# A sandwich layer of linear attention and a mixture of experts on one core: GpSimd's double power behind the fourth key sums, VectorE's x_mid behind the candidate mask and xn1

## What is computed

```python
# block 1: linear attention in chunks of 128, mixed with a memory
q, k, v = h @ w_q.T, h @ w_k.T, h @ w_v.T
sq, sk = elu(q) + 1, elu(k) + 1
mem   = (sq @ memory) / clip(sq @ memory_norm, EPS)
A     = (sq_chunk @ sk_chunk.T) * causal
local = (A @ v + sq_chunk @ S) / clip(A.sum(-1) + sq_chunk @ z, EPS)   # S += sk.T @ v, z += sk.sum
out   = (g * mem + (1 - g) * local) @ w_o.T
# block 2: 1024 experts chosen by product keys, 4 heads, 8 of them each, and a dense part
sim           = queries of h against 64 keys a side and head
sx, sy        = top 8 of each side;  scores = top 8 of the 64 sums sx + sy
w             = silu((h . down_embed[idx]) * softmax(scores))
out           = sum(w * up_embed[idx]) + silu(h @ W_up.T) @ W_down.T
```

## Time and profile before

| | us |
|---|---|
| median of 3 runs | 2862.96 |
| lowest, highest | 2859.02, 2871.89 |
| the profiled execution, its own time | 2859.55 |
| its span | 2857.8 |
| PE busy | 2784.0 (97%) |
| PEld busy | 2178.7 (76%) |
| DVE busy | 2624.6 (92%) |
| ACT busy | 2539.0 (89%) |
| POOL busy | 2064.3 (72%) |

### The profile page before, as it was taken

The page is one execution under the profiler, slowest core; times in us unless marked ns, Lnnn a source line. Parts: engine busy times, 40 slices in busy tenths (PEclk is TensorE's granted clock), DMA queues, the critical chain, the costliest instruction groups (busy, mean ns, idle before and its releaser), DMA issues.

```text
span 2857.8 us, 46700 instructions
## 1 busy us (share of the span) xinstructions
PE 2784.0 (97%) x13306; PEld 2178.7 (76%) x13306; DVE 2624.6 (92%) x6346; ACT 2539.0 (89%) x3692; POOL 2064.3 (72%) x2435
## 2 busy tenths in 40 slices
PE   8999999999999999999999999999999999999998
PEld 7677777777777777777777777777777777777776
DVE  6899899999999999999999999999999999999986
ACT  6888989899899898998998989989989889899997
POOL 5666677777777777777777777777777777777774
PEclk9999999999999999999999999999999999999999
DMA  4787888788878887888788778877887788788764
GB/s 133 151 168 159 170 170 170 162 173 172 168 161 175 167 172 158 174 172 168 160 176 171 165 166 173 169 164 168 171 173 162 169 173 173 159 176 171 147 152 117
DMA packets 609029, 471.49 MB, mean 165 GB/s; under 512 B 362371, under 2 KB 543492, under 8 KB 608772
## 3 DMA queue, kind: packets, MB, share of 16 engines
q0 software_dynamic: 52832, 199.77, 39.6%
q1 hardware_dynamic: 555940, 268.74, 38.3%
HBM read 137.37 MB, written 131.20 MB: 94 GB/s over the span
## 4 chain that ended last, share of the span: by engine, by line
DVE 46%; PE 19%; ACT 13%; issue 13%; POOL 8%; DVEq 0%; POOLq 0%; ACTq 0%
PE banks L873 17%; DVE sums L1402 5%; DVE banks L1405 4%; DVE prob_odd L1443 4%; DVE picked L1392 4%; DVE prob_odd L1549 4%; DVE w_blocks L1477 4%; DVE xn L1338 3%; POOL sums L696 3%; ACT L1190 3%; ACT prob_odd L1213 3%; DVE picked L1541 2%; POOL wexp L772 2%; DVE x_mid L1568 2%; DVE top L1492 1%
## 5 line engine op out<-in xcount | busy, mean ns | idle before, releaser
L696 POOL TENSOR_TENSOR sums<-scores 128x1024 f32<-128x1024 f32 x512 | 1066.4, 2085 | 327.6 <-ACT scores L1304 320.4
L873 PE MATMUL banks<-deT,xn2T 128*128 128x512 f32 x1024 | 481.9, 593 | 5.5 <-DVE wexp L1423 4.9
L873 PE MATMUL banks<-xn2T,wupT 128*128 128x256 f32 (+1 forms) x2272 | 465.3, 359 | 3.5 <-DVE state L1536 2.5
L873 PE MATMUL banks<-ue,gT 128*128 128x256 f32 x2048 | 462.9, 379 | 2.3 <-ACT gT L1234 2.3
L873 PEld LDWEIGHTS banks<-ue,gT 128*128 128x128 f32 x2048 | 388.8, 190 | 55.3 <-ACT gT L1234 2.7
L873 PEld LDWEIGHTS banks<-xn2T,wupT 128*128 128x128 f32 x2272 | 390.1, 191 | 46.6 <-DVE state L1536 3.3
L873 PEld LDWEIGHTS banks<-deT,xn2T 128*128 128x128 f32 x1024 | 184.6, 190 | 138.4 <-issue 123.4
L1549 DVE SCALAR_TENSOR_TENSOR prob_odd<-picked,rz,prob_odd 128x1024 f32<-128x1024 f32 x128 | 257.6, 2012 | 18.5 <-ACT prob_odd L1213 12.7
L1170 ACT ACTIVATE wexp<-prob_odd 128x1024 f32<-128x1024 f32 x127 | 134.2, 1057 | 154.1 <-DVE w_blocks L1477 153.7
L714 POOL TENSOR_TENSOR cprob<-cmask,cdif 128x112 f32<-128x112 f32 x128 | 58.7, 459 | 263.7 <-DVE cmask L1574 263.7
L873 PE MATMUL banks<-route,xn2T 128*128 128x512 f32 x512 | 240.8, 592 | 0.8 <-ACT xn2T L1134 0.8
(11 more groups left out here) (191 smaller groups left out, 7393.1 us busy)
## 6 DMA issues: line engine op xcount, KB each, us to landing
wexp<-wexp POOLq DMA_DIRECT2D x127, 1024.0 KB, 10.4
wexp<-wexp POOLq DMA_DIRECT2D x127, 512.0 KB, 5.2
w_way<-w_blocks SPq DMA_DIRECT2D x127, 512.0 KB, 3.1
g_parts<-w_way SPq DMA_DIRECT2D x508, 128.0 KB, 7.6
xn_way<-xn_blocks SPq DMA_DIRECT2D x992, 32.0 KB, 1.7
x_in<-_attn_hidden_states_dram SPq DMA_DIRECT2D x128, 128.0 KB, 5.9
out_dram<-x_out SPq DMA_DIRECT2D x128, 128.0 KB, 8.3
xn1T<-xn_way SPq DMA_DIRECT2D x125, 128.0 KB, 3.9
```

The lines of the kernel that those rows point to most:

```text
L696: return nc.gpsimd.tensor_tensor(sums[:, k, :, :], scores[:, k, 0:XIN].unsqueeze(2).broadcast_to([P, XIN, NKEYS]), scores[:, HEADS + k, :] ...
L873: last = nc.tensor.matmul(out, lhs(c), rhs(c), start=(start and c == 0), stop=(stop and c == chunks - 1), skip_group_check=shared)
```

## The change

On POOL the fourth sums (head 3) go ahead of the power and of its waits. On DVE the candidate mask and xn1 go ahead of x_mid. Computation, tiles and semaphores are the same.

```diff
--- before.py
+++ after.py
@@ -699,6 +699,8 @@
                                                ALU.add)
 
             def body(t, steady):
+                if t[9] is not None:
+                    key_sums(3).then_inc(s_head_3_sums_ready, 1)
                 if t[7] is not None:
                     pool.wait_ge(s_mix_var_eps, t[7] + 1)
                     if with_y(t[7]) is None:
@@ -706,8 +708,6 @@
                     else:
                         pool.wait_ge(s_y_var_eps, with_y(t[7]) + 1)
                         two_powers(2 * LN_O + t[7] % 2, 2 * LN_Y + with_y(t[7]) % 2).then_inc(s_mix_rstd, 1)
-                if t[9] is not None:
-                    key_sums(3).then_inc(s_head_3_sums_ready, 1)
                 if t[9] is not None:
                     pool.wait_ge(s_cand_exp_ready, t[9] + 1)
                     pool.wait_ge(s_cand_mask_ready, t[9] + 1)
@@ -1562,14 +1562,6 @@
                     x_moments(x)
                 if seven(t[13]) and t[13] % 2 == 0:
                     cross_added(t[13])
-                if t[7] is not None:
-                    dve.wait_ge(s_mix_rstd, t[7] + 1)
-                    wait(dve, s_x_out_ready, t[7] - MID_SLOTS + 1)
-                    nc.vector.scalar_tensor_tensor(x_mid[:, t[7] % MID_SLOTS, :], mix[:, 0:D], rstd[:, LN_O, t[7] % 2:t[7] % 2 + 1],
-                                                   x_in[:, t[7] % SLOTS, :], ALU.mult, ALU.add).then_inc(s_x_mid_ready, 1)
-                    if t[7] == 1:
-                        dve.wait_ge(s_ue_in, 16)
-                        nc.vector.reduce_sum(ue_sum[:, :], ue[:, :, :], axis=AX.X).then_inc(s_ue_cent, 1)
                 if t[9] is not None:
                     nc.vector.tensor_tensor(cmask[:, :, :], cand_out, per_head(best[:, :, TOP - 1], NCAND), ALU.is_ge).then_inc(s_cand_mask_ready, 1)
                 x = ahead(t, 4)
@@ -1587,6 +1579,14 @@
                         x_stats(x + 2)
                         x_moments(x + 2)
                         x_eps(x + 2)
+                if t[7] is not None:
+                    dve.wait_ge(s_mix_rstd, t[7] + 1)
+                    wait(dve, s_x_out_ready, t[7] - MID_SLOTS + 1)
+                    nc.vector.scalar_tensor_tensor(x_mid[:, t[7] % MID_SLOTS, :], mix[:, 0:D], rstd[:, LN_O, t[7] % 2:t[7] % 2 + 1],
+                                                   x_in[:, t[7] % SLOTS, :], ALU.mult, ALU.add).then_inc(s_x_mid_ready, 1)
+                    if t[7] == 1:
+                        dve.wait_ge(s_ue_in, 16)
+                        nc.vector.reduce_sum(ue_sum[:, :], ue[:, :, :], axis=AX.X).then_inc(s_ue_cent, 1)
 
             pipeline(body)
```

## The result

The changed kernel takes 2913.28 us (median of 4 runs, 2912.14 to 2916.21) against 2861.83 for the kernel before in the same comparison: ratio 1.0175, 95% interval 1.0149 to 1.0201. It is slower by 51 us, inside the range given (2822 to 2975), but not the forecast: it is rival 1 in its partial form. The profiled execution has a span of 2911.5 us at full granted clock; DVE is busy 2670.3 us (92%), POOL 2244.1 (77%), PE 2794.9 (96%).

A forecast was written before the change was run, and what follows sets the result against it. A loop through POOL's head-pair DMA (L772) was taken to bound the step, so DVE's -0.3 + 0.25 - 0.23 us hardly counts; 4 us off 2859.55 gives 2855.5, median 2859, forecast 2855. Range for 8 in 10: 2822 to 2975.

The forecast's parts named there:

- rival 1: DVE's x_mid is held by POOL's third sums: +190 us, about 3050, or near 2990; chance 0.28.
- partial form: x_mid is held by the third sums in some steps only: +20 to +110 us; a third of the 0.28.
- The loop through the DMA: POOL's head-pair DMA (L772) and its landing set the step; 0.15 us in two steps can go.
- the sum: Whole run: 0.15 us in two steps, about 55 times, 8 us at most, half taken: 4 us.
- (a): POOL's fourth sums ahead of the power shorten DVE's L1549: between 0 and -0.68 us, taken as -0.3.
- (c): DVE's L1402 moves later and no longer meets POOL's third sums: 0.23 us a step gained.
- (b): x_mid behind cmask and xn1 on DVE, with rstd ready: +0.1 to +0.3 us, taken as +0.25.
- The full one: x_mid is held by the third sums in every step: about 3050, or near 2990; chance 0.2.
- The Trainium skill's rule: DVE and POOL share a port pair; who starts first locks it; alone, the sum would be 87 us less.
- the signs named: Profile after: L1549 1.3 to 1.4 or near 2.0, L1402 1.27, `xn` above 0.6, L1063's wait 35 to 50 us.
- the two that the text called fatal: Forecast wrong if x_mid's mean exceeds 0.9 us or the two-step loop is outside 43.0 to 43.7.

The follow-up runs named there:

- experiment 6: The changed kernel with POOL's third sums waiting for x_mid and the DMA L772 over half its columns, against the kernel before: 2801.07 us, ratio 0.9783.
- experiment 3: The changed kernel with POOL's third sums made to wait for x_mid, against the kernel before: 2843.93 us, ratio 0.9949.
- experiment 4: The changed kernel with cmask behind xn1 on DVE (xn1, cmask, x_mid), against the kernel before: 2847.11 us, ratio 0.9958.
- experiment 10: The changed kernel with a 4-column sum added on GpSimd between cprob and the third sums, against the kernel before: 2851.67 us, ratio 0.9958.
- experiment 8: The changed kernel with the two short additions of `cross_added` moved behind x_mid, against the kernel before: 2993.68 us, ratio 1.0455.
- experiment 11: The kernel before with GpSimd's power for x moved behind the issue of the DMA L772, against the kernel before: 2898.26 us, ratio 1.0126.

## Why the prediction was wrong

**The loop through the DMA** was right: the landing is where it was, and experiment 6 shows it to be the bound of experiment 3's form, in which x_mid is free. It caps the gain as the text had it: no form of the change that does all the work had a median below 2843.9, though L1549 and L1402 give 111 us. The size was too small: without the contest the change gives 16 us (experiment 3), where the sum had 4 and 8 at most. In the profiled executions 5 us of it are there by the eleventh L772, at 289 us, a stretch that the sum left out; from there on a pair of steps gains 0.20 us, where the sum had 0.15.

**(a)** was taken as -0.3 and measured -0.64 us, close to its bound of -0.68: L1549 gets in front of the power as a rule, even where the power's row starts first. That each order eats most of the gain was an assumption with no row.

**(c)** was right: 0.23 taken, 0.23 measured.

**(b)** is the step that failed, with the "rstd is ready (the power ends by 1217.1 in the worse order, x_mid starts near 1217.4)". The end was right: 1.89 us behind L1549's start, as L644 at 1236.45 against 1234.56. But x_mid's start was worked out with an L1549 only 0.3 us shorter. With (a) in full, cmask starts 1.24 behind L1549 and x_mid would start 0.52 later, at 1.76, which is 0.13 before the power's end. (a) and (b) were costed as if they were independent, and the gain of the one is what puts x_mid on the edge of the other. The 0.52 us behind cmask became 0.67, the lead on the third sums 0.15 instead of 0.31, and the term of +0.25 became +2.0 in about half the steps.

**Rival 1** had the mechanism, the place and nearly the price: x_mid ends 0.31 behind the third sums (0.29 in the text) and lasts 2.50. "It decides when the sums ask for the port before x_mid does" fits experiments 3, 4 and 10, in which x_mid goes first once the sums come later; the asking itself no row shows. What was set against it, that the sums' row starts 0.3 behind x_mid, is true only of the steps in which x_mid doesn't wait. Its two forms were given 0.28 in all, and the partial one, +20 to +110, a third of that; it came at +51. The full one's "near 2990 if (a) gives its full 0.68" does not come out of its own terms: 1.6 less 0.68 over 118 steps is 109 us, near 2970. The `cross_added` of every second step, which puts 0.5 us between L1549 and cmask and so lets the power end first, stood in the code and was not weighed.

**The Trainium skill's rule** (SBUF — State Buffer, section "SBUF: two separate sides"), that the engine which starts first has the shared port pair, was read on the starts of rows. This case's rows do not allow that reading: x_mid at 1236.48 starts ahead of the sums at 1236.63 and loses, with a lead of up to 0.16 us in some 60 steps, while in experiment 10 it wins against the short sum at that same lead. The rule may still hold of the moment at which the port is asked for, which no row shows.

**Of the signs named:** L1549 1.37, L1402 1.31, `xn` of x_mid 0.70, L719 on the DMA in 121 rounds, all as forecast; x_mid's mean of 1.51 (limit 0.9) and 44.69 for two steps (limit 43.7) are the two that the text called fatal. L1063's wait of 88.9 lies between the forecast's 35 to 50 and rival 1's 150.

## What to carry over

Where two engines hold each other off at their inputs, work out the new start of an instruction from its own releaser as well as from its row of neighbours, after all gains that lie ahead of it are booked; an edge of 0.15 us can decide 2 us. A wait added on the engine that has slack, or even a short useless instruction, can be worth more than the move itself: check the order of arrival, not only the load. The wait cost GpSimd 45.2 us of idling here and nothing in the step. And a gap in front of a DMA's issue is not free room if that transfer is on the loop that sets the step.

## What the runs showed of the hardware

- The order in which two rows start does not say which of the two instructions is held. A two-input DVE instruction (x_mid) that came up while GpSimd was in cprob lost to the 1024-column sums behind it at a lead of 0.17 us or less, though its row started first, and won from 0.18 on (two early steps each in the changed kernel and in experiment 8; the others there from 0.32); against a 4-column sum behind cprob it won at 0.16.
- Such a DVE instruction ends 0.29 us behind the GpSimd instruction that held it, be that cprob, the sums or another (x_out behind L693).
- Instructions of one or two elements a partition are held as fully as long ones: L644 (2 elements) has a mean of 2.089 us beside L1549 against 1.061, and starts before the instruction that holds it.
- Taking a short power (a row of 0.5 us) from in front of a DMA's issue on GpSimd brought the issue 0.11 us forward and delayed the sums behind it by 0.43 (medians of experiment 11).
